# TensorE's loop body of the recurrent steps: sixteen steps and eight gate blocks in place of four and two

## The chip, the cores and the metric

The kernel runs on one core of a Trainium2 chip. Its time is the device time of one execution in microseconds (us), taken as the median of several. The core has five engines with a program each: TensorE (PE, matmuls; PEld is its weight load), VectorE (DVE), ScalarE (ACT), GpSimd (POOL) and SyncE (SP, which issues the DMAs here). They meet only through semaphores.

## The reference

Four layers in a row, each added to its input `x` of shape (4, 512, 512): batch, time, feature.

```python
x = x + attention(rms_norm(x) * (1 + scale) + shift)       # 16 heads, scale and shift from cond
x = x + gru(cond, x)                                        # hidden state starts at cond
x = x + causal_conv(x, cond)                                # depthwise, 4 taps
x = x + (causal_conv(x, cond) + b)

def cell(h, x):                                             # 512 steps, one after the other
    gi = x @ W_ih + b_ih
    gh = h @ W_hh + b_hh
    r = sigmoid(i_r + h_r); z = sigmoid(i_z + h_z)
    n = tanh(i_n + r * h_n)
    return (1 - z) * n + z * h
```

All is float32. The GRU can't be parallel in time: each of its 512 steps needs the state of the step before.

## The kernel before

**Stages.** The first block of the program does attention for the four batches, and the gate inputs `gi = x @ W_ih` for the first 128 time steps. It takes about 611 us. The second block does the 512 recurrent steps, and beside them the gate inputs for the other 384 time steps.

**A recurrent step.** TensorE multiplies the state `h` (128 partitions, 4 batches, 4 chunks of features) with `W_hh`, whose output columns are cut into four groups of 32 array columns (`NG`), in two halves `h` = 0 and 1 of the features. `products` (line 1100) issues the matmuls of one gate set, one half and two chunks: line 1106. A float32 matmul of the program appears in the profile as two matmuls with a weight load each, so 64 of the program are 128 in the trace. VectorE then transposes the sums (lines 962 and 968), ScalarE takes sigmoid and tanh (1064, 1070, 1075), VectorE scans (974 and 979) and so writes the next state, for which TensorE waits at the start of the next step (line 1111, `s_h`). ScalarE puts the input part of the next step into PSUM (`seed_rn`, `seed_z`), for which TensorE waits too. GpSimd does both convolutions two steps at a time.

**Gate blocks.** The remaining gate inputs are cut into `NBLOCKS` = 184 blocks of 104 columns. A block is computed in two halves, one behind each of two steps: `part(v, q)` (line 1126), eight matmuls of the program at line 1134, sixteen in the trace. SyncE brings each half's operands and counts them in `s_pair[v]`, VectorE takes the finished block (`take`) and counts `s_taken`. So the first 368 steps carry a part and the last 144 don't.

**Order and loops.** Every engine has its program written out by hand, in the order of the code. VectorE's 368 steps with blocks are written out in full, its last 144 are a loop of two steps a pass. ScalarE loops over sixteen steps, GpSimd over two. TensorE has two loops (`Fori` is a loop that the engine runs itself, with a counter in a register and a branch at the end of the body): the first over the steps with gate blocks (line 1143), the second over the rest (line 1149). Times of waits are computed from the counter (`e.snap` puts a value into a register).

Of the kernel before, what the change touches and what calls it, by code (L numbers as in the profile page):

```python
# [30 lines left out]
def build(nc, x, vec, w_emb, w_qk, w_v, w_out, w_rz, w_n, w_hh, b_rz, out):  # L31
    with ExitStack() as ctx:
# [820 lines left out]
        NBLOCKS = len(BLOCKS)  # L853
# [25 lines left out]
        def h_of(u, h):  # L879
            return hb[:, u, h, 0:HS].rearrange("p (i s) -> p i s", s=3)[:, :, 2]  # L880
# [11 lines left out]
        with nc.Block() as block:  # L892
# [200 lines left out]
            @block.tensor  # L1093
            def _(e):
                wv = whh[:].rearrange("p c (q G n) -> p c q G n", q=3, G=NG)

                def step(t, u):
                    half = (e.snap(2 * t + 1), e.snap(2 * t + 2))

                    def products(dst, gates, h, k2):  # L1100

                        n = len(range(3)[gates]) * 64
                        for k in (2 * k2, 2 * k2 + 1):
                            hv = h_of(u, k // 2).rearrange("p (b c) -> p b c", c=2)[:, :, k % 2]
                            for G in range(NG):
                                last = e.matmul(bank[dst[h]][32 * G:32 * G + B, 0:n], hv,  # L1106
                                                wv[:, k, gates, G, 64 * h:64 * h + 64],
                                                start=False, stop=k2 == 1 and k == C - 1, skip_group_check=True)
                        return last
                    rn, z = slice(0, 3, 2), slice(1, 2)  # L1110
                    e.wait_ge(st["s_h"], half[0])
                    e.wait_ge(st["s_seed_rn"], half[0])
                    products(RN, rn, 0, 0)
                    e.wait_ge(st["s_seed_rn"], half[1])
                    products(RN, rn, 1, 0)
                    e.wait_ge(st["s_h"], half[1])
                    products(RN, rn, 0, 1).then_inc(st["s_rn"], 1)
                    e.wait_ge(st["s_seed_z"], half[0])
                    products(RZ, z, 0, 0)
                    products(RZ, z, 0, 1).then_inc(st["s_z"], 1)  # L1120
                    products(RN, rn, 1, 1).then_inc(st["s_rn"], 1)
                    e.wait_ge(st["s_seed_z"], half[1])
                    products(RZ, z, 1, 0)
                    products(RZ, z, 1, 1).then_inc(st["s_z"], 1)

                def part(v, q):

                    if v == 0:
                        e.wait_ge(st["s_taken"], e.snap(q + 1))
                    e.wait_ge(s_pair[v], e.snap(q * 32 + 32))  # L1130
                    for k in (2 * v, 2 * v + 1):
                        for g in range(NG):
                            rows = slice(32 * g, 32 * g + 32)
                            last = e.matmul(bank[FB][rows, 0:BW], fixed[:, k, rows], moving[:, k, :],  # L1134
                                            start=k == 0, stop=k == C - 1)
                    last.then_inc(st["s_part"], 1)

                e.wait_ge(st["s_clear"], N_CLEAR)
                for b in RN + RZ:
                    for G in range(NG):  # L1140
                        last = e.matmul(bank[b][32 * G:32 * G + B, 0:P], zero[:, 0:B], zero, start=True, stop=True)  # L1141
                last.then_inc(st["s_open"], 1)
                with e.Fori(0, NBLOCKS // 2) as it:
                    for w in range(2):
                        q = e.snap(it * 2 + w)
                        for v in range(2):
                            step(q * 2 + v, v)
                            part(v, q)
                with e.Fori(NBLOCKS, T // 2) as it:
                    for v in range(2):  # L1150
                        step(it * 2 + v, v)
# [97 lines left out]
```

## Time and profile before

| | us |
|---|---|
| median of 3 runs | 2217.25 (2214.75 to 2222.03) |
| the profiled execution | 2214.76 |
| its span | 2212.8 |
| start of the first recurrent step | 617.87 |
| end of the first loop, start of the second | 1766.65 |
| TensorE busy | 2126.4 (96%) |
| VectorE, ScalarE, GpSimd busy | 1389.0, 1186.0, 1134.9 |

The span is the time from the first to the last instruction of the profiled execution. Busy time counts instructions that do work; register, branch and semaphore instructions aren't in it. A chain of waits is the work that ended last, followed back step by step; a piece called "issue" is time in which the engine waited for nothing that the profile shows. Instruction code has DMA queues of its own, which the page lists as "instruction".

### The profile page before, as it was taken

Reading aid. Unit: us, or ns where it says so; the run is one execution under the profiler, and the core shown is the slowest. Engines: PE = TensorE matmul, PEld = TensorE weight load, DVE = VectorE, ACT = ScalarE, POOL = GpSimd, SP = SyncE. Lnnn points to the kernel's source line nnn. Section 1 sums busy time; section 2 is a strip of 40 time slices with the busy share of each in tenths; the row PEclk is TensorE's granted clock in tenths of the full one; section 3 lists DMA queues with packets and bytes.
Section 4 is the critical chain, followed back from the end, with each engine's and each line's share of the span. In section 5 each row is a group of like instructions: output and inputs, shape, how many; then the busy total and the mean of one; then the engine's idle time right before and its main releaser. Section 6 shows DMA issues by size and latency. Waiting matters only on the chain.

```text
span 2212.8 us, 184515 instructions
## 1 busy us (share of the span) xinstructions
PE 2126.4 (96%) x76736; PEld 1590.4 (72%) x76736; DVE 1389.0 (63%) x5092; ACT 1186.0 (54%) x5992; POOL 1134.9 (51%) x3895
## 2 busy tenths in 40 slices
PE   6899999999989999999999999999999999999997
PEld 1222222222379999999999999999999988888886
DVE  1444443444257777777777777777777777777775
ACT  2344444443245555555555555555555555565554
POOL 1142432433135556555555656556555666666665
PEclk9899999999999999999999999999999999999999
DMA  6000000001022222112222221122221100000000
GB/s 247 1 1 1 1 1 1 1 20 59 32 58 51 54 54 51 49 51 53 68 52 52 54 53 49 50 70 55 50 51 50 48 5 24 6 6 5 5 7 19
DMA packets 159135, 86.69 MB, mean 39 GB/s; under 512 B 126016, under 2 KB 154944, under 8 KB 158272
## 3 DMA queue, kind: packets, MB, share of 16 engines
q1 hardware_dynamic: 158896, 83.42, 14.0%
q10 hardware_dynamic: 144, 2.10, 0.2%
q8 instruction: 48, 0.79, 0.1%
q14 instruction: 47, 0.39, 0.1%
HBM read 26.37 MB, written 12.58 MB: 18 GB/s over the span
## 4 chain that ended last, share of the span: by engine, by line
PE 66%; DVE 4%; issue 1%; DMA 1%; POOL 0%; ACT 0%; POOLq 0%; SPq 0%; DVEq 0%
PE ps L1106 60%; PE ps L1134 6%; DVE arena L962 3%; DVE arena L979 1%; DMA arena<-arena 1%; POOL arena L1171 0%; ACT ps L1039 0%; DVE arena L968 0%; PE ps L1141 0%; DVE arena L974 0%; POOL arena L1175 0%; POOL arena L1177 0%; DVE arena L1011 0%; DVE seq L992 0%; ACT arena L1070 0%
## 5 line engine op out<-in xcount | busy, mean ns | idle before, releaser
L1106 PE MATMUL ps<-whh,arena 128*4 128x128 f32 (+1 forms) x65536 | 1452.7, 246 | 34.2 <-DVE arena L979 27.2
L1106 PEld LDWEIGHTS ps<-whh,arena 128*4 128x4 f32 x65536 | 1310.3, 87 | 157.5 <-DVE arena L979 77.9
L962 DVE STREAM_TRANSPOSE arena<-ps 128x128 f32<-128x128 f32 x1024 | 434.7, 425 | 250.0 <-PE ps L1106 249.7
L1064 ACT ACTIVATE arena<-arena 128x8 f32<-128x8 f32 x1024 | 215.6, 211 | 649.5 <-DVE arena L962 628.0
L1171 POOL TENSOR_TENSOR arena<-tap,seq 128x32 f32<-128x32 f32 x1024 | 231.5, 257 | 256.3 <-DVE seq L992 256.3
L381 DVE TENSOR_REDUCE top<-ps 128x2 f32<-128x1024 f32 x128 | 150.8, 1220 | 257.5 <-PE ps L620 257.5
L979 DVE TENSOR_TENSOR_SCAN arena<-arena 128x24 f32<-128x24 f32 x1024 | 214.6, 210 | 144.8 <-ACT arena L1075 144.8
L1039 ACT ACTIVATE ps<-arena 128x128 f32<-128x128 f32 x1026 | 269.8, 263 | 0.7 <-PE ps L1141 0.7
L1171 POOL TENSOR_TENSOR arena<-tap,arena 128x32 f32<-128x32 f32 x1024 | 231.3, 257 | 66.8 <-POOL arena L1181 66.8
L968 DVE STREAM_TRANSPOSE arena<-ps 128x64 f32<-128x64 f32 x1024 | 253.2, 247 | 10.8 <-PE ps L1106 1.5
L523 PE MATMUL ps<-arena 128*32 128x512 f32 x2048 | 246.0, 600 | 11.5 <-POOL arena L214 11.5
L222 POOL TENSOR_TENSOR arena<-arena 128x2048 f32<-128x2048 f32 x16 | 72.8, 4551 | 337.0 <-ACT arena L296 337.0
L1075 ACT ACTIVATE arena<-arena 128x16 f32<-128x16 f32 x1024 | 222.7, 217 | 7.4
L974 DVE TENSOR_TENSOR_SCAN arena<-arena 128x16 f32<-128x16 f32 x1024 | 217.7, 213 | 4.8
L1175 POOL TENSOR_TENSOR arena<-arena 128x64 f32<-128x64 f32 x512 | 164.1, 320 | 95.2 <-POOL arena L1171 95.2
L1070 ACT ACTIVATE arena<-arena 128x8 f32<-128x8 f32 x1024 | 202.5, 198 | 1.1 <-DVE arena L968 1.1
L1134 PE MATMUL ps<-arena 128*32 128x104 f32 x5888 | 199.7, 253 | 1.7 <-DMA arena<-arena 1.7
L296 ACT ACTIVATE arena<-ps 128x1024 f32<-128x1024 f32 x128 | 124.1, 1022 | 133.5 <-PE ps L696 132.4
L523 PEld LDWEIGHTS ps<-arena 128*32 128x32 f32 x2048 | 60.2, 110 | 173.1 <-issue 173.1
L1043 ACT ACTIVATE ps<-arena 128x64 f32<-128x64 f32 x1026 | 181.6, 209 | 0.0
L1177 POOL TENSOR_TENSOR arena<-arena 128x32 f32<-128x32 f32 x512 | 129.0, 252 | 93.9 <-POOL arena L1175 93.9
L1134 PEld LDWEIGHTS ps<-arena 128*32 128x32 f32 x5888 | 131.8, 109 | 2.1 <-DMA arena<-arena 2.1
(89 smaller groups left out, 1298.9 us busy)
## 6 DMA issues: line engine op xcount, KB each, us to landing
arena<-arena SPq DMA_DIRECT2D x240, 104.0 KB, 2.1
arena<-seq SPq DMA_DIRECT2D x128, 104.0 KB, 2.1
arena<-gi_d SPq DMA_DIRECT2D x256, 32.0 KB
gi_d<-arena SPq DMA_DIRECT2D x108, 52.0 KB, 1.6
seq<-in_x SPq DMA_DIRECT2D x4, 1024.0 KB, 17.1
arena<-arena SPq DMA_DIRECT2D x32, 128.0 KB, 2.1
whh<-in_w_hh SPq DMA_DIRECT2D x1, 3072.0 KB, 21.2
arena<-seq SPq DMA_DIRECT2D x24, 128.0 KB, 2.2
```

What stands on the lines that cost most here:

```text
L523: last = e.matmul(dst[rows], w[:, rows], v, start=start, stop=stop)
L962: e.transpose(trn[:, h].rearrange("p q (i c s) -> p q c i s", c=2, s=2)[:, :, :, :, 0], bank[RN[h]][:, 0:P].rearrange("p (q c i) -> p q c ...
L968: e.transpose(trz[:, h].rearrange("p (i c) -> p c i", c=2), bank[RZ[h]][:, 0:64].rearrange("p (c i) -> p c i", c=2)).then_inc(st["s_tr"], 1)
L974: e.tensor_tensor_scan(pre[:, h], r_d0[:, h], trn[:, h, 1, 0:2 * NH], 0.0, ALU.mult, ALU.add).then_inc(st["s_pre"], 1)
L979: e.tensor_tensor_scan(hb[:, 1 - u, h, 0:HS], z_d0[:, h], hb[:, u, h, 1:HS + 1], 0.0, ALU.mult, ALU.add).then_inc(st["s_h"], 1)
L1039: e.activation(bank[RN[h]][:, 0:P].rearrange("p (q n) -> p q n", q=2), at(19456 + SLOT * s + 64 * h, 512).rearrange("p (q w) -> p q w", q= ...
L1064: e.activation(r_d0[:, h].rearrange("p (i s) -> p i s", s=2)[:, :, 1], trn[:, h, 0, 0:2 * NH].rearrange("p (i s) -> p i s", s=2)[:, :, 0], ...
L1070: e.activation(z_d0[:, h].rearrange("p (i s) -> p i s", s=3)[:, :, 2], trz[:, h, 0:NH], ACT.Sigmoid)
L1075: e.activation(hb[:, u, h, 1:HS + 1].rearrange("p (i s) -> p i s", s=3)[:, :, 0:3:2], pre[:, h].rearrange("p (i s) -> p i s", s=2)[:, :, 1 ...
L1106: last = e.matmul(bank[dst[h]][32 * G:32 * G + B, 0:n], hv, wv[:, k, gates, G, 64 * h:64 * h + 64], start=False, stop=k2 == 1 and k == C - ...
L1134: last = e.matmul(bank[FB][rows, 0:BW], fixed[:, k, rows], moving[:, k, :], start=k == 0, stop=k == C - 1)
L1171: last = e.tensor_tensor(prd[:, 0, w * k:w * k + w].rearrange("p (i s) -> p i s", s=2), tap[:, k], src[:, :, bass.ds(t + k, 2)], ALU.mult)
```

## The change

The first loop of TensorE's program runs over sixteen steps and eight blocks a pass, 23 passes, in place of four steps and two blocks, 92 passes. `step` and `part` and the numbers that they wait for are the same, and so is the second loop.

```diff
-                with e.Fori(0, NBLOCKS // 2) as it:
-                    for w in range(2):
-                        q = e.snap(it * 2 + w)
+                with e.Fori(0, NBLOCKS // 8) as it:
+                    for w in range(8):
+                        q = e.snap(it * 8 + w)
                         for v in range(2):
                             step(q * 2 + v, v)
                             part(v, q)
```

The programs of the other four engines are unchanged. On TensorE, before, this stands at the end of a pass, in and behind the fourth step (a row is a line, an instruction, its output and inputs, its shape and how often it follows itself; the semaphores are those of the text above):

```order
L1106 MATMUL ps<-whh,arena 4x128 x8
L1106 MATMUL ps<-whh,arena 4x64 [waits s_seed_z]
L1106 MATMUL ps<-whh,arena 4x64 x15
L1134 MATMUL ps<-arena 32x104 [waits s_pair1]
L1134 MATMUL ps<-arena 32x104 x7
L1143 REGISTER_ALU
L1143 COMPARE_AND_BRANCH
```

Behind the fourth step's block part the counter is raised and the branch goes back to the first step of the body.

On TensorE, now, at the same place, behind the fourth step:

```order
L1106 MATMUL ps<-whh,arena 4x128 x8
L1106 MATMUL ps<-whh,arena 4x64 [waits s_seed_z]
L1106 MATMUL ps<-whh,arena 4x64 x15
L1134 MATMUL ps<-arena 32x104 [waits s_pair1]
L1134 MATMUL ps<-arena 32x104 x7
L1111 ISA
L1106 MATMUL ps<-whh,arena 4x128 [waits s_seed_rn,s_h]
L1106 MATMUL ps<-whh,arena 4x128 x7
L1114 REGISTER_ALU
L1106 MATMUL ps<-whh,arena 4x128 [waits s_seed_rn]
```

The fifth step follows at once, and the counter and the branch stand behind the sixteenth. The written-out body is four times as long.

## Rows read from the trace of the kernel before

**Rows 1.** The page, part 1: busy us (share of the span) and instructions of each engine.

```profile
PE 2126.4 (96%) x76736; PEld 1590.4 (72%) x76736; DVE 1389.0 (63%) x5092; ACT 1186.0 (54%) x5992; POOL 1134.9 (51%) x3895
```

**Rows 2.** The page, part 5: groups by line, count | busy, mean ns | idle before.

```profile
L1106 PE MATMUL ps<-whh,arena 128*4 128x128 f32 (+1 forms) x65536 | 1452.7, 246 | 34.2 <-DVE arena L979 27.2
...
L1134 PE MATMUL ps<-arena 128*32 128x104 f32 x5888 | 199.7, 253 | 1.7 <-DMA arena<-arena 1.7
```

**Rows 3.** Busy us of PE, PEld, DVE, ACT, POOL; clock, DMA, GB/s; loop, passes 2 on.

```profile
633.95:1766.65 1132.70, 1125.78 (x52416) 1049.42 (x52417) 824.82 (x3459) 660.68 (x4004) 677.54 (x2729) 1.00 0.21 53
```

**Rows 4.** Timeline of TensorE, one pass: start us, us, instructions [idle before].

```profile
646.42 2.83 PE L1106 MATMUL ps<-whh,arena 128*4 128x128 f32 x128
...
649.47 2.83 PE L1106 MATMUL ps<-whh,arena 128*4 128x128 f32 x128
...
652.48 2.83 PE L1106 MATMUL ps<-whh,arena 128*4 128x128 f32 x128
...
655.49 2.84 PE L1106 MATMUL ps<-whh,arena 128*4 128x128 f32 x128
...
658.75 1.50 PE L1106 MATMUL ps<-whh,arena 128*4 128x128 f32 x48
```

**Rows 5.** Chain of waits, first pass of the first loop: start us, us, what.

```profile
617.87 4.58 PE ps L1106 x128
...
622.81 1.67 PE ps L1106 x69
624.48 0.02 issue
624.50 1.22 PE ps L1106 x54
625.72 0.35 PE ps L1134 x15
626.07 1.47 PE ps L1106 x52
627.54 0.47 issue
628.00 1.45 PE ps L1106 x70
...
630.83 0.69 issue
631.52 0.65 PE ps L1106 x16
```

**Rows 6.** DMA queues, first pass (617.87 to 633.95): packets, MB, share.

```profile
q8 instruction: 4, 0.07, 1.6%
```

**Rows 7.** DMA queues, the 91 passes that follow (633.95 to 1766).

```profile
q1 hardware_dynamic: 141235, 60.07, 21.0%
q14 instruction: 38, 0.31, 0.1%
```

**Rows 8.** DMA queues, start of the second loop (1766 to 1780).

```profile
q8 instruction: 2, 0.03, 1.1%
```

**Rows 9.** DMA queues, a stretch of the attention stage (100 to 400).

```profile
q8 instruction: 21, 0.34, 0.5%
```

**Rows 10.** Busy time of the same stretch, columns as in rows 3.

```profile
100.00:400.00 300.00, 292.81 (x2650) 80.86 (x2648) 127.81 (x138) 145.31 (x200) 105.96 (x30) 0.99 0.01 1
```

**Rows 11.** Busy time by stretch, around two idle times, columns as in rows 3.

```profile
66.40:69.47 3.07, 0.00 (x1) 0.03 (x1) 2.94 (x6) 0.00 (x0) 0.00 (x0) 0.86 0.00 0
68.60:78.80 10.20, 7.89 (x48) 2.55 (x52) 4.97 (x25) 2.54 (x3) 0.00 (x0) 0.50 0.00 1
610.85:615.49 4.64, 0.00 (x0) 0.00 (x1) 1.15 (x9) 1.17 (x5) 0.00 (x0) 0.92 0.21 40
615.49:621.50 6.01, 5.52 (x120) 3.89 (x124) 0.42 (x1) 2.54 (x8) 0.00 (x0) 0.50 0.53 92
621.50:633.95 12.45, 11.15 (x496) 9.91 (x489) 7.54 (x34) 6.09 (x39) 3.77 (x15) 1.00 0.13 35
```

## Prediction

> **What bounds the kernel now.** I read the page first: TensorE is busy 96% of the span [rows 1]. The reader is to see one engine that sets the pace and is almost never idle, so what happens between its instructions counts. The groups by line say of what its work in the recurrent steps consists: 65536 matmuls of line 1106 in 512 steps are 128 a step, 5888 of line 1134 in 368 steps are 16 a step [rows 2], and each has a weight load of its own. A step with a gate block's part is thus 288 matmuls and weight loads.
>
> Next comes the stretch of the loop that the change touches. From its second pass to its end, 91 passes take 1132.70 us [rows 3], 12.447 us for four steps. With the first pass, which begins at 617.87 [rows 5] and ends at 633.95, the loop takes 1148.8 us, half the span.
>
> Then the timeline of one pass. Steps start at 646.42, 649.47, 652.48, 655.49 and, across the branch, 658.75 us [rows 4]: 3.05, 3.01, 3.01 and 3.26 apart. So the branch with its register work costs 0.25 us of TensorE's time, and the rest of the loop is dense.
>
> Last, the very first pass, in which the body's code is new. Its chain has pieces called "issue", in which TensorE waited for nothing that the profile shows: one ends at 624.50, one at 628.00 (0.47 us long), one at 631.52 (0.69 us) [rows 5]. They lie 3.50 and 3.52 us apart, and some 121 matmuls of the chain (54, 15 and 52) with as many loads lie between two of them. In the same 16 us the instruction queue q8 moved 4 packets, 0.07 MB [rows 6]; in the 91 passes that follow q8 has no row [rows 7], and at the start of the next loop it moved 2 packets [rows 8]. In a stretch of the attention stage 21 packets go with 2650 matmuls and 2648 loads, 252 instructions to a packet, and 0.34 MB over 21 is 16 KB [rows 9, 10]. So TensorE's code comes in blocks of 16 KB, about 256 instructions; code that is there already is not fetched again; and new code comes one block at a time: a front that ran further ahead would have had the whole slow attention stage (a block in 14 us) to get there, and the first pass would not have stopped at each border.
>
> **The change, part by part.** Only TensorE's program changes. It does the same 184 blocks and 368 steps in 23 passes of sixteen steps in place of 92 passes of four.
>
> Removed: 69 branches at 0.25 us are 17.3 us, if nothing else happened.
>
> Added: size of the body. The present one has 4 x 288 = 1152 matmuls and loads and about 18 waits and register instructions, 1170 in all, 4.6 blocks. Where it begins within a block follows from the first pass: up to the stop at 624.48 stand 128 + 16 + 69 matmuls [rows 5], with their loads 426 instructions, and some five others, 431; one border lies 256 earlier, 175 after the body's start. The body starts some 80 instructions into a block and touches 5 blocks. The new body has 4608 and about 66, 4674 instructions; it ends 4754 instructions, 18.57 blocks, after the start of its first block, and touches 19.
>
> Whether 19 blocks stay at hand no row shows; 5 do. I take it that they don't: nothing in this trace was ever held in that amount, and a front that fetches only the next block looks like one over a small store. If blocks are dropped in the order in which they came, a store shorter than the body holds the wrong ones at each turn, and all 19 are fetched in every pass.
>
> The Trainium skill has a figure for this in "Runtime: NRT & Kernel Launch", section "Instruction fetch mechanics": 128 KiB for TensorE, 2048 instructions, in blocks of 16 KiB. The trace agrees on the block; that 8 blocks are the limit no row shows, and by it a body of 4674 would not fit.
>
> What a new block costs: TensorE uses up 256 instructions in 12.447 x 256 / 1170 = 2.72 us, and a new block comes 3.50 us after the one before. The fetch is the slower, so a pass goes at the pace of the fetches and each border costs 0.78 us. The bounds for a block: 2.72 us (the fetch just hidden), and 3.66 us (from the border 175 instructions into the first pass, which by that step's 4.94 us for 292 instructions lies at 620.8, to 624.5). I take 3.50, which the rows show twice. The work of the other engines lies beside this: VectorE, ScalarE, GpSimd and SyncE keep their programs, wait for TensorE's semaphores and have slack (the first three are busy 58 to 73% of this stretch [rows 3]); a wait for them of a tenth or three falls into the 0.78 us.
>
> What the jump back costs: its target is 18 blocks behind and has to be fetched with nothing beside it. No row has such a jump. The nearest is again one full fetch, 3.50 us. Below it stands 0.25 us, the jump of today. Above it: the block behind the loop was asked for when the last block was entered; the loop leaves that block after 146 instructions, 1.5 us, so if fetches queue up the jump waits the other 2.0 us and then 3.50, 5.5 us.
>
> The sum of a pass: 18 borders x 3.50 = 63.0 us and the last piece 1.5, together 64.5; 23 passes 1483.5. Jumps back: 22 x 3.50 = 77.0. Together 1560.5 us.
>
> The clock: after idle times of 3.07 and 4.64 us TensorE's granted clock was 0.50, the 1.2 GHz level, for 10 and for 6 us [rows 11]. A jump leaves it idle for about 3.5 us, so I expect such a fall in most passes. At that level a block takes 4.94 x 256 / 292 = 4.33 us in place of 3.50; over 6 us that is 1.4 blocks x 0.83 = 1.15 us a pass, 26 us in 23. Bounds: 0 (no fall) and 45 us (10 us in each pass).
>
> The loop then takes 1586.5 us and took 1148.8: +438 us. The profiled execution took 2214.76 us (the span and 2.0 outside it), which makes 2653 us; the median of the runs shown is 2.5 us higher than it, which I leave out. That is 20% slower.
>
> **A rule that speaks otherwise.** The same section of the Trainium skill says that the prefetch keeps ahead, because instructions are issued more slowly than blocks come, and that a taken branch to code that isn't there stalls. By the rows blocks came more slowly than they were used (3.50 against 2.72 us). By the rule alone the sum would be that of the second rival; by the rows it is mine.
>
> **The rivals.**
> 1. All 19 blocks stay at hand. Then 17.3 us go, and in the first pass 14 more blocks are new, at 0.78 us 10.9: 2214.8 - 17.3 + 10.9 = 2208 us. It decides as soon as the store is as long as the body. For it: no loop's code was fetched twice in this trace. Against it: that store is almost four times what is shown. This is the case on the other side, 0.3% faster, at the very border. Chance 0.06.
> 2. Borders are hidden once TensorE runs warm (the gaps belong to the cold start), and only the jump costs: 2214.8 - 92 x 0.25 + 22 x 3.50 = 2269 us, with clock falls 2295. For it: the clock was 0.50 in the first 3.6 us of that pass. Against it: the gaps grew, 0.02, 0.47, 0.69, after it had risen [rows 5, 11]. Chance 0.07.
> 3. The store keeps some blocks through the turn, say 8 of 19: 11 borders and the jump a pass, 23 x (11 x 0.78 + 3.5) - 23 = +255, 2470 us. Nothing speaks for a rule by which it would; nothing excludes it. Chance 0.05.
> 4. My forecast, every block in every pass: chance 0.82. Its own range: with 3.3 us a block and no fall of the clock 2539, with 3.6 us, queued jumps of 5.6 us and long falls 2759.
>
> **How the numbers follow.** The likeliest case gives 2653 us. The range runs from 2535 to 2765; it holds nearly all of that case and leaves out the three rivals, 0.18. A change under 0.3%, 7 us, can't be told from none. Rival 1 is split over that border: faster 0.03, same 0.03. All else is slower, 0.94.
>
> **What would show it.** q8 would have 480 to 510 packets and some 8 MB in place of 48 and 0.79. In the loop TensorE would have "issue" gaps of 0.7 to 0.8 us some 3.5 us apart, and every 66 to 71 us one gap of 3.5 to 5.5 us, behind which its granted clock is 0.50. Its busy share of the span would fall to about 80%. The stretch behind the loop, some 438 us, would be as before, and so would the counts of the groups. I am wrong if q8 stays near 60 packets (rival 1), if it has 480 and yet the steps between two jumps start 3.0 us apart (rival 2), or if it has 250 to 350 (rival 3). If the gaps at the borders are right and the jump's is 1 or 8 us, only that term was off.

## The result, and the profile after

The changed kernel takes 2768.3 us (median; 2766.4 to 2776.4) against 2217.0 (2214.8 to 2222.0), a ratio of 1.249 with a 95% interval of 1.246 to 1.252. The forecast was 2653, its range up to 2765, so the time lies 3 us outside.

The page after, parts 1, 3 and 4 (columns as in the page before; a queue's row is packets, MB, share):

```profile
PE 2240.8 (81%) x76736; PEld 1653.5 (60%) x76736; DVE 1368.4 (50%) x5092; ACT 1179.3 (43%) x5992; POOL 1135.5 (41%) x3895
...
q8 instruction: 502, 8.22, 1.3%
...
PE 56%; issue 16%; DVE 4%; ACT 1%; POOL 0%; POOLq 0%; DVEq 0%
```

TensorE is busy 81% of the span where it was 96% [rows 1], with the same 76736 matmuls. The instruction queue moved 502 packets in place of 48, and 16% of the chain that ended last is "issue". Per pass that is (502 - 48) / 23, about 20 packets: the 19 blocks of the body and the one behind it. Between any two jumps the trace has 20.

Busy time by stretch after, the whole first loop, and the second loop (columns as in rows 3):

```profile
618.66:2317.00 1698.34, 1254.09 (x52992) 1125.27 (x52992) 812.75 (x3492) 660.85 (x4046) 682.32 (x2745) 0.97 0.16 40
```
```profile
2316.80:2755.00 438.20, 409.35 (x18453) 363.58 (x18443) 311.35 (x1303) 259.96 (x1591) 268.24 (x1080) 1.00 0.04 8
```

The first loop takes 1698.3 us and took 1148.8, 549.5 more, which is all but 2 us of the difference of the spans (2764.4 less 2212.8, 551.6). The second loop takes 438 us as before.

The chain of waits after, around one jump back (start us, us, what), to be held against the first pass before [rows 5]:

```profile
743.86 2.83 PE ps L1106 x128
746.69 1.22 issue
747.91 0.56 PE ps L1134 x16
748.47 2.40 PE ps L1106 x109
750.87 1.03 issue
751.91 0.45 PE ps L1106 x18
...
754.87 0.89 issue
755.76 0.78 PE ps L1106 x30
...
758.73 1.23 issue
759.96 0.77 PE ps L1106 x22
...
762.15 3.26 issue
765.41 4.48 PE ps L1106 x128
769.89 0.36 PE ps L1134 x16
770.25 1.65 PE ps L1106 x69
771.89 0.18 issue
772.07 1.22 PE ps L1106 x54
...
775.11 1.02 issue
```

The pattern of the first pass before is now that of every pass: a stop after each 256 instructions. Here the stops end 4.00, 3.85 and 4.20 us apart (747.91, 751.91, 755.76, 759.96). Behind 759.96 TensorE works off what the loop has in its last block, other engines finish the step's chain, and the rest is the jump: the first step of the next pass starts at 765.41. By the trace's record of the branch, TensorE hangs on it for 4.07 us here and for 4.32 in the mean of the 22 jumps. Its first 213 matmuls stand before the stop at 771.89, as they did at 624.48.

The granted clock, in a part of the time at the jump, and behind it (columns as in rows 3):

```profile
761.20:765.20 4.00, 0.30 (x15) 0.07 (x3) 1.01 (x5) 1.09 (x7) 1.72 (x7) 1.00 0.20 46
765.70:769.10 3.40, 3.40 (x89) 3.05 (x84) 0.69 (x3) 0.38 (x2) 1.52 (x7) 0.50 0.19 33
```

After the idle 4 us the clock was at the 1.2 GHz level for 3.4 us here. It fell in all 22 passes that begin with a jump, in 13 of them for 3.4 us and in 9 for 6.8.

### The profile page after: what moved, and what is told of

Same layout as the page of the kernel before. It is cut to its first block, busy times and chain, and to the rows that moved or that the text cites. A ratio compares the mean times of both kernels' runs of the same rounds, so it can differ in the third digit from the quotient of the medians.

```text
span 2764.4 us, 184377 instructions
## 1 busy us (share of the span) xinstructions
PE 2240.8 (81%) x76736; PEld 1653.5 (60%) x76736; DVE 1368.4 (50%) x5092; ACT 1179.3 (43%) x5992; POOL 1135.5 (41%) x3895
## 3 DMA queue, kind: packets, MB, share of 16 engines
q1 hardware_dynamic: 158896, 83.42, 11.3%
## 4 chain that ended last, share of the span: by engine, by line
PE 56%; issue 16%; DVE 4%; ACT 1%; POOL 0%; POOLq 0%; DVEq 0%
PE ps L1106 51%; PE ps L1134 5%; DVE arena L962 3%; DVE arena L979 1%; ACT ps L1039 0%; ACT arena L1070 0%; ACT arena L1075 0%; DVE arena L968 0%; DVE arena L974 0%; ACT arena L1064 0%; PE ps L1141 0%; POOL arena L1171 0%; DVE arena L1011 0%; POOL arena L1175 0%; POOL arena L1177 0%
## 5 line engine op out<-in xcount | busy, mean ns | idle before, releaser
L1106 PE MATMUL ps<-whh,arena 128*4 128x128 f32 (+1 forms) x65536 | 1581.9, 250 | 420.9 <-issue 369.1
L1106 PEld LDWEIGHTS ps<-whh,arena 128*4 128x4 f32 x65536 | 1378.7, 88 | 586.4 <-issue 464.6
L1134 PE MATMUL ps<-arena 128*32 128x104 f32 x5888 | 227.7, 256 | 51.5 <-issue 51.5
L974 DVE TENSOR_TENSOR_SCAN arena<-arena 128x16 f32<-128x16 f32 x1024 | 195.7, 191 | 4.7
L1134 PEld LDWEIGHTS ps<-arena 128*32 128x32 f32 x5888 | 151.5, 111 | 60.9 <-issue 60.9
L523 PEld LDWEIGHTS ps<-arena 128*32 128x32 f32 x2048 | 60.2, 110 | 173.2 <-issue 173.2
```

What stands on the lines that cost most here:

```text
L523: last = e.matmul(dst[rows], w[:, rows], v, start=start, stop=stop)
L974: e.tensor_tensor_scan(pre[:, h], r_d0[:, h], trn[:, h, 1, 0:2 * NH], 0.0, ALU.mult, ALU.add).then_inc(st["s_pre"], 1)
L1106: last = e.matmul(bank[dst[h]][32 * G:32 * G + B, 0:n], hv, wv[:, k, gates, G, 64 * h:64 * h + 64], start=False, stop=k2 == 1 and k == C - ...
```

## The experiments

Theory A: code comes in blocks of 256 instructions, one at a time, slower than TensorE uses them up; the store holds 8 blocks; a body that needs more is fetched anew in each pass. Its rivals are that only the jump costs, that the store is larger, and, for the size of the effect, that the kernel's own transfers slow the fetch.

**How many blocks stay: e1, e2, e11, e3, e4.** The six-step body needs one block written out behind the loop, since 184 is not a multiple of 3:

```diff
-                with e.Fori(0, NBLOCKS // 8) as it:
-                    for w in range(8):
-                        q = e.snap(it * 8 + w)
+                with e.Fori(0, NBLOCKS // 3) as it:
+                    for w in range(3):
+                        q = e.snap(it * 3 + w)
                         for v in range(2):
                             step(q * 2 + v, v)
                             part(v, q)
+                for v in range(2):
+                    step(2 * (NBLOCKS - 1) + v, v)
+                    part(v, NBLOCKS - 1)
```

> Body of six steps and three blocks, 61 passes, and the 184th block written out behind the loop: 1754 instructions that begin some 80 slots into a fetch block, so 8 blocks are touched and a ninth is asked for while the eighth runs. Theory A (the store holds 8 blocks, and the oldest goes first, the block fetched ahead included): each pass loses its first block to the ninth, and the whole body is fetched anew each time: per pass 7 borders x 3.8 + 0.6 + 4.3 = 31.5 us against 18.65, so 2217 + 61 x 12.9 = about 3000 us, q8 some 550 packets. Rival B (the store is larger, 9 to 18 blocks, and only the 19 of the changed kernel do not fit): no refetch, 31 branches fewer at 0.25 us, about 2210 us, q8 some 55 packets.

e2 and e11 are e1 with tiny matmuls at the start of the program, 46 and 30 of them, which move the body within its blocks:

```diff
                 e.wait_ge(l_vec, 16)
+                for _ in range(46):
+                    e.matmul(bank[OB][0:B, 0:B], vecT[:, 0, 0:B], vecT[:, 0, 0:B], start=True, stop=True)
                 e.wait_ge(l_emb, 16)
```

> The same body of six steps, with 46 tiny matmuls (184 instructions) added at the program's start, where TensorE waits for its first weights, so that the body begins about 8 slots into a fetch block and touches 7 blocks; with the one fetched ahead that makes 8. Theory A (8 blocks in all): all of it fits, no block is fetched twice, 2217 - 31 x 0.25 = about 2209 us, q8 some 56 packets. If the store holds only 7, it is as slow as the run beside it. Rival B: the same 2209, and the run beside it too. A difference between the two runs is a matter of blocks alone, since the instructions of the loop are the same.

> The body of six steps again, with 30 tiny matmuls (120 instructions) at the program's start, so that it begins some 200 slots into a block: it touches 8 blocks as in e1, but the eighth holds 162 of its instructions and not 42. In e1 only every other pass fetched its code anew (30 long jumps in 60). Theory A (the request for the ninth block pushes the first out, and in e1 the jump often came before that request was made, since only 42 instructions lay between): here every pass fetches all 8 blocks, 7 x 3.8 + 0.6 x 2.72 + 4.6 = 33 us a pass, 2217 + 61 x 14.2 = about 3080 us. Rival (something else drops the first block every other time): about 2570 us again.

e3 and e4 have 4 and 1 in place of 8 in the changed lines.

> Body of eight steps and four blocks, 46 passes: 2338 instructions, 10 blocks touched. Theory A (store of 8): all fetched in every pass, 9 borders x 3.8 + 1.2 + 4.3 = 39.7 us against 24.9 of now: 2217 + 46 x 14.8 = about 2895 us, slower than the sixteen-step body although it has more straight code, q8 about 510 packets. Rival B (store of 10 to 18): 2217 - 46 x 0.25 = 2206 us. Rival C (the jump back alone costs, borders are cheap once warm): 2217 - 23 + 45 x 4.3 = 2388 us.

> Body of two steps and one block, 184 passes, 586 instructions, 3 blocks touched. By every theory all code stays at hand and only the price of the branch shows: 92 more of them at 0.25 us, 2217 + 23 = 2240 us.

| run | steps a pass | blocks touched | us | ratio (95%) | q8 packets | long jumps of all |
|---|---|---|---|---|---|---|
| before | 4 | 5 | 2220.3 | 1 | 48 | 0 of 91 |
| e4 | 2 | 3 | 2231.2 | 1.005 (1.0035 to 1.0066) | 46 | 0 of 183 |
| e2 | 6 | 7 | 2216.5 | 0.998 (0.9973 to 0.9991) | 54 | 0 of 60 |
| e1 | 6 | 8 | 2569.5 | 1.157 (1.156 to 1.159) | 323 | 30 of 60 |
| e11 | 6 | 8 | 3005.7 | 1.356 (1.353 to 1.358) | 593 | 60 of 60 |
| e3 | 8 | 10 | 2849.1 | 1.283 (1.281 to 1.285) | 548 | 45 of 45 |
| after | 16 | 19 | 2768.3 | 1.249 | 502 | 22 of 22 |

The queue's row on the pages of e2, e1 and e11, whose loops hold the same instructions:

```profile
q8 instruction: 54, 0.88, 0.2%
```
```profile
q8 instruction: 323, 5.29, 0.9%
```
```profile
q8 instruction: 593, 9.72, 1.4%
```

The store holds 8 blocks, one of which the request ahead takes: a body in 7 blocks runs without a fetch, the same body in 8 doesn't, and the difference is 789 us between e2 and e11. Rivals B and C of e3 are out: C had 2388 us. Fewer steps a pass cost more once the body doesn't fit (e11, e3, after: 3006, 2849, 2768), and with them goes the number of jumps (60, 45, 22); e3 and after have the same 414 borders inside their passes, and 45 jumps of 4.62 us against 22 of 4.32. e1 missed: I expected about 3000 us, and every other pass ran from the store. e11 took 3006 us where I expected 3080.

The traces show what makes the difference. In e1 the body leaves 38 instructions in its eighth block (by the start at 76 that e12 shows below), in e11 158. Here are a pass of e1 with stops and the one behind it, first their rows of the instruction queue (663.9 to 694; from 694 to 712.4 the queue has no row), then two places of the chain:

```profile
q8 instruction: 9, 0.15, 2.4%
```
```profile
692.94 0.97 issue
693.91 0.23 PE ps L1109 x2
...
713.61 3.72 issue
```

Behind the last stop, at 693.91, the branch follows after 0.19 us. No packet for a ninth block is seen, and the branch finds its target. The pass behind it, 18.4 us, fetches nothing: all 8 blocks are there. It has no stop at its end, and there the packet of the ninth block does come, 0.44 to 0.59 us after the branch begins; this branch doesn't find its target (4.49 to 4.99 us, 4.74 in the mean). So it goes in all of the 60 jumps, in turn. In e11 the branch comes 1.19 us after the last stop, the ninth block's packet starts about when the branch does (0.04 us before it in the mean), and no jump finds its target. That the request for the ninth block throws out the first is how this fits together; the trace has no record of what the store drops.

**The jump back: e5, e6.** e5 writes all 184 blocks out (`for q in range(NBLOCKS)`, no loop). e6 adds a hint to the changed kernel:

```diff
-                with e.Fori(0, NBLOCKS // 8) as it:
+                with nc.Fori(0, NBLOCKS // 8, engines=bass.OrderedEngineSet([e.engine]), hint_back_edge=True) as it:
```

> The 368 steps with blocks are written out, with no loop and no jump: 106.6 thousand instructions, 417 fetch blocks. Theory (the fetch of one block at a time sets the pace, 3.8 us a block in the changed kernel's run): 416 x 3.8 = 1581 us for the stretch, so 2768 less 22 jumps of about 4.4 us = 2670 us, q8 about 465 packets, and no fall of the clock inside. Rival (the borders are slow only because each pass begins with a miss and a half clock, straight code would catch up): the stretch comes near 368 x 3.04 = 1119 us, 2190 us in all.

> The changed kernel with a hint at the top of the body which names the branch at its end, so that the branch's target can be fetched before it is taken. If the hint works across 18 blocks, the jump's 4.4 us shrink to under 1 and the kernel takes 2768 - 22 x 3.8 = about 2685 us; the borders stay at 3.8. If the hint is lost on the way or the fetched block is pushed out again: 2768.

e5 took 2609.6 us (ratio 1.176), with 460 packets. Straight code does not catch up, so rival 2 of the prediction is out. Its chain, from the middle of the stretch (start us, us, what):

```profile
1501.91 0.88 issue
1502.80 2.43 PE ps L1109 x95
...
1505.57 0.69 issue
1506.27 0.38 PE ps L1137 x5
1506.64 2.55 PE ps L1109 x116
1509.19 0.91 issue
1510.11 0.29 PE ps L1109 x6
```

The stops are there without any loop: they end at 1502.80, 1506.27 and 1510.11, and the packets start 3.70 us apart in the mean. Both this and the 60 us that e5 is below what I expected say that a block takes 0.1 to 0.15 us less here than in the changed loop. e6 took 2731.6 us, 37 less than the change, where I expected 83 less: the record of the branch shows 2.60 us a jump in place of 4.32, 38 us in 22 jumps. Its chain at a jump:

```profile
762.49 1.69 issue
764.19 4.48 PE ps L1106 x128
```

What a jump consists of can be read from the packets of q8 around it. Here are the queue's rows at one jump of the changed kernel (760.5 to 765) and at one of e15 (688 to 692), the same loop with only 14 instructions in its last block:

```profile
q8 instruction: 2, 0.03, 3.5%
```
```profile
q8 instruction: 1, 0.02, 1.6%
```

In the changed kernel one packet is that of the block behind the loop, which starts 0.09 us after the branch (means of 22 jumps); the target's starts 1.02 us after the branch, takes 1.89, and TensorE goes on 1.40 after its end: 4.32 us with rounding. In e15 there is only the target's packet. It starts 1.03 us after the branch, takes 1.10, and TensorE goes on 1.40 later: 3.53 us. So the block behind the loop doesn't hold back the start of the target's packet, it makes it slower, by 0.8 us; in e12, where it starts 0.80 us ahead of the branch, the target's takes 1.22 us, and in e1, 0.52 us behind the branch, 2.01. In e6 a pass has 19 packets in place of 20, the one of the block behind the loop is missing, and the target's starts 0.10 us after the branch and takes 1.06. The hint thus saves the 0.9 us until the packet starts and the 0.8 by which it was slower, and leaves the rest.

**The time of a block: e7 to e10.** e7 brings the operands of the gate blocks once, e8 also loads the ring only for the first sixteen steps:

```diff
                     weights, src = wn[:, ks, P * b:P * b + P], seq_cb[:, ks, c, PAD + a:PAD + a + BW]
+                    if q:
+                        e.sem_inc(s_pair[v], 32)
+                        return
...
-                    load_ring(e, first // HALF % 2, first)
+                    e.sem_inc(s_ring[first // HALF % 2], 16 * NG)
```

> The changed kernel, but the operands of the gate blocks are brought once, for block 0, and all later blocks use them again (their values are wrong by that); of the loop's small packets most are gone, the ring loads and stores stay. Theory A (a block took 3.8 us and not 3.5 because its packet stands behind the kernel's own transfers): intervals fall to about 3.45, 23 x 18 x 0.35 = 145 us less, about 2620 us. Rival (3.8 is what the fetch costs in this stretch, whatever else moves): 2768.

> As the run beside it, and the ring of gate inputs is loaded only for the first sixteen steps and used again after (values wrong by that). What stays are the stores of the blocks. Theory A: intervals fall to about 3.35, about 2580 us. Rival: 2768.

They took 2742.9 and 2743.3 us, 25 us less than the change, not the 145 and 190 of theory A. Between packet starts stand 3.79 and 3.78 us in the mean, 3.86 in the changed kernel: the transfers taken out (q1 has 44656 and 35728 packets in place of 158896) cost 0.07 us a block. The stores of the blocks stay in both.

e9 and e10 put the fetch by itself behind the last step of the kernel before:

```diff
+                with e.Fori(0, 10) as it:
+                    for j in range(1168):
+                        G = j % NG
+                        e.matmul(bank[5][32 * G:32 * G + B, 0:64], zero[:, 0:B], zero[:, 0:64], start=True, stop=True)
```

> The kernel before, and behind its last step TensorE runs 10 passes over a body of 1168 matmuls of the 4x64 form (4672 instructions, as many as the changed body) that wait for nothing and multiply zeros into a bank that nobody reads. This measures the fetch by itself: no waits, hardly any transfers. In the changed kernel the interval between two fetches was 3.86 us, 3.6 to 3.7 at borders in the first two thirds of a step and 4.0 to 4.2 near its end. Theory A (the waits for the state, at a step's start, hold up the request for the next block): all intervals here 3.55 to 3.65, no pattern, the jump back 4.2 us; a pass 18 x 3.6 + 5 = 70 us. Rival B (3.86 is what a fetch costs): 3.86 throughout, 74 us a pass. Rival C (the pattern belongs to the blocks and their place in memory): intervals of 3.6 and 4.1 here too.

> The same body cut into sixteen steps of 72 matmuls; at a step's start TensorE waits for VectorE, which is let go by the step's 48th matmul and then makes two transposes (some 0.9 us). Theory A: at borders that lie in the last third of a step the next request comes later, by 0.3 to 0.5 us, at the others not; mean 3.7 to 3.8. Theory B or C: as the run beside it, the step's start makes no difference.

The chain of e9, in one of its passes:

```profile
2279.17 2.81 PE ps L1155 x128
2281.99 0.93 issue
2282.92 1.97 PE ps L1155 x128
2284.89 1.50 issue
2286.39 1.97 PE ps L1155 x128
2288.36 1.51 issue
2289.86 1.97 PE ps L1155 x128
```

128 matmuls and 128 loads, then a stop, and so on: a block is 256 instructions to the last one. The starts are 3.47 to 3.75 us apart; between the 199 packets the mean is 3.60 us and the median 3.51, 5% are below 3.34 and 5% above 4.04. That is the fetch with no wait and next to no transfer beside it, as theory A had it. It has three parts, by the traces' means: 1.16 us from TensorE's going on in a new block to the start of the next one's packet, 1.06 for the packet, 1.38 from its end until TensorE goes on. Rival B (3.86 here too) and C (a pattern) are out; the means by place in the pass lie between 3.50 and 3.70, but for the first behind the jump (3.20). A pass took 71.7 us, where 70 were expected, and the jump 3.39, not 4.2. (e9 and e10 were run once each, 2918.5 and 2915.7 us; what is read here is inside their traces.) In e10 the mean is 3.66; borders that lie 200 to 250 instructions into a step have 3.79, the others 3.57 to 3.73. The effect of a wait is there but smaller than the 0.3 to 0.5 us I expected.

**Where a border lies: e15.** The changed kernel with 32 of the tiny matmuls.

> The changed kernel with 32 tiny matmuls (128 instructions) at the program's start: the same body begins half a block later. In the changed kernel the intervals between fetches were long (4.0 to 4.2 us) behind the blocks 6 to 8 and 15, 16 of a pass, whose borders lie in the last third of a step. If the place in the step decides (each border lies 36 instructions earlier in its step than the one before), the long ones move 3 to 4 blocks on, to some 2 to 4 and 10 to 12. If the block's place in memory decides, they stay. The sum hardly changes: 2768, with one block more or less 3.8 us x 23 = up to 90 us either way; by the count the body now ends at 204 + 4674 = 4878, 19.05 blocks, so it touches 20: some 2780.

It took 2786.5 us, where 2780 was expected. The mean intervals behind the fetches 2 to 4 of a pass (the first is the one behind the jump's) were 4.09, 3.91 and 3.96 us, and behind 11 to 13 3.99, 3.81 and 3.94; between the groups 3.6 to 3.8. In the changed kernel the long ones are 6 to 8 (4.03, 4.03, 4.01) and 15 to 17 (4.17, 4.04, 3.98). So the time of a block goes with its place in the step. One long interval doesn't fit, the 11th with 3.98; it is 3.72 and 3.61 in e7 and e8, so it belongs to the kernel's own transfers. In e5, where each block runs once, the same is seen, but weaker: 3.60 to 3.66 us at borders 75 to 200 instructions into a step, 3.76 to 3.79 behind that. Of the three parts of a fetch only one grows at those places of the changed kernel: the next block's packet starts 1.44 to 1.64 us after TensorE went on, and 1.12 to 1.37 at the others that follow a full stop. What holds the request up isn't shown: e10 speaks for the wait at the step's start, and for a part of it only.

**A version that beats both: e12, e13, e14.** e2 is 3.8 us faster than before by 31 branches fewer, e4 10.9 slower by 92 more. That looks like 0.12 us for each branch removed or added, which I took as its price. In the turned loop the branch stands inside a step, behind its first two groups of matmuls:

```diff
+                step(0, 0, rest=False)
                 with e.Fori(0, NBLOCKS // 2) as it:
                     for w in range(2):
                         q = e.snap(it * 2 + w)
                         for v in range(2):
-                            step(q * 2 + v, v)
+                            step(q * 2 + v, v, first=False)
                             part(v, q)
+                            step(q * 2 + v + 1, 1 - v, rest=False)
```

(`rest=False` issues `products(RN, rn, 0, 0)` and `products(RN, rn, 1, 0)` with their waits, `first=False` the others; behind the loop the begun step is completed, one more step follows, and the second loop begins two steps later. e14 is this. e12 and e13 are the same with three blocks a pass and 28 and 30 tiny matmuls at the start.)

> A version meant to beat both: six steps a pass in 7 blocks (28 tiny matmuls at the program's start place the body), and the loop is turned, so that the branch stands behind the first two groups of matmuls of a step (64 instructions of the 128-column form) and not behind a gate block part at the step's end. Where the branch is now, TensorE has about 28 instructions in its queue, 0.2 us, and the branch with its register work takes 0.47. Theory (with 64 wide instructions queued, 0.8 us, the branch is hidden): 60 x 0.25 = 15 us less than the run e2, ratio to before 0.991, 2200 us. Rival (the queue is no fuller there): 0.998, as e2.

> e12 again with the body at the right place. Its first long stop in each pass lay 2 instructions behind the body's first one: the body began at slot 253 and touched 8 blocks, since my count of the start (80) was 4 too high. Now 30 tiny matmuls in place of 28: slot 5, 7 blocks, no refetch, q8 some 55 packets. The price of a branch by e2 and e4 is 0.12 us (3.8 us for 31, 11 for 92) and not 0.25. If turning the loop hides it, 60 x 0.12 = 7 us less than e2: ratio to before 0.995. If it does not, 0.998. If a branch there costs more, since its register work now stands inside a step, 1.000 or above.

> The kernel before with its loop turned in the same way (branch behind the first two groups of matmuls of a step), 92 passes of four steps, nothing moved otherwise: the price of the branch alone. Hidden: 92 x 0.12 = 11 us less, ratio 0.995. Not hidden: 1.000.

e12 took 3046.5 us, with 593 packets and 60 long jumps in 60 passes: it began at slot 253, three before a block's end, and touched 8 blocks. My count of 80 for the start was 76 in truth. e13, two tiny matmuls more, took 2195.7 us (0.989, 0.9875 to 0.9908), and e14 2189.9 us (0.9866, 0.9850 to 0.9883): the best version, 31 us below the kernel before where 11 were expected, and simpler than e13, which gains nothing from its longer pass. The step starts of e14, by its timeline, and behind them those of the kernel before, in the same 14 us of the loop:

```profile
1001.92 2.83 PE L1109 MATMUL ps<-whh,arena 128*4 128x128 f32 x128
...
1004.94 2.83 PE L1109 MATMUL ps<-whh,arena 128*4 128x128 f32 x128
...
1007.94 2.84 PE L1109 MATMUL ps<-whh,arena 128*4 128x128 f32 x128
...
1010.96 2.84 PE L1109 MATMUL ps<-whh,arena 128*4 128x128 f32 x128
```
```profile
1000.44 2.83 PE L1106 MATMUL ps<-whh,arena 128*4 128x128 f32 x128
...
1003.47 2.83 PE L1106 MATMUL ps<-whh,arena 128*4 128x128 f32 x128
...
1006.70 2.83 PE L1106 MATMUL ps<-whh,arena 128*4 128x128 f32 x128
...
1009.80 2.83 PE L1106 MATMUL ps<-whh,arena 128*4 128x128 f32 x128
...
1012.86 1.40 PE L1106 MATMUL ps<-whh,arena 128*4 128x128 f32 x44
```

In e14 the steps are 3.00 to 3.02 us apart here. In the kernel before, the step across the branch takes 3.23 and those behind it 3.10 and 3.06. Its branch is recorded at 1006.20; the first matmul behind it starts 0.31 us after the last one ahead of it, while around e14's branch at 999.39 no two matmuls start more than 0.11 us apart.

The price of a branch follows from whole passes. A pass of e2 (six steps) takes 18.49 us in the mean and one of the kernel before (four) 12.45; the two steps more are 3.02 us each, and 12.45 less 4 x 3.02 leaves 0.37 us for the branch, 34 us in 92. A pass of e14 takes 12.12, so its branch costs about 0.04 (a pass of e4, 6.31, leaves 0.27 for the branch), and 92 x 0.33 = 30 us is what e14 gains. The 0.12 was too low because e2 pays for its longer body elsewhere: its loop is only some 7 us shorter by the traces, where 31 branches are worth 11. Its first six steps and the two written out behind the loop take 4 us more than in the kernel before; there the code is new, 54 packets in all against 48. Whether it is the wide matmuls in the queue or the distance from the wait at the step's start that hides e14's branch, no run separates.

## Why the prediction came out as it did

The mechanism was right, and the forecast failed by the size of a term, the time of a new block; the jump was sized too low as well, and the clock too high.

- *Every block in every pass.* Right: 502 packets where 480 to 510 were forecast. The limit that no row of before showed is now shown: 7 blocks and the one ahead.
- *Stops at the borders, 0.7 to 0.8 us, some 3.5 us apart.* They are there, but 0.9 to 1.2 us long and further apart. This is the step that failed: "I take 3.50, which the rows show twice". The loop's 1698.3 us, less 22 jumps of 4.32 and 23 last pieces of 1.5, leave 3.79 us for each of its 414 borders. 0.29 x 414 is 120 us. Two stops were read as if a fetch had one length. e9 shows what it has: a median of 3.51 us, which the two stops met, but 3.60 in the mean with a spread from 3.34 to 4.04, and a sum over 414 borders goes by the mean. To that come 0.07 us for the transfers (e7) and, as an estimate from the long intervals of the changed kernel (six of the 19 in a pass, some 0.3 us above the others), about 0.1 for the borders near the end of a step. My own upper bound of 3.66 was below the measured mean, too.
- *The jump, 3.50 us.* Measured 4.32, between the bounds of 3.50 and 5.5: 18 us more. The step that was wrong is that the target is fetched "with nothing beside it": the packet of the block behind the loop is under way, and the target's takes 1.89 us with it and 1.10 without (e15, where the jump takes 3.53). The upper bound, fetches that queue up one behind the other, is out: the target's packet starts 1.02 us after the branch either way.
- *The clock, 26 us.* It falls as forecast, in each pass, but that costs little or nothing: behind the jump shown above, at half clock for 3.4 us, TensorE comes from its first matmul (765.41) to the second border (772.07) in 6.66 us, less than two borders at 3.79. A block at half clock needs about as long as the fetch beside it, so the stop is only shorter (0.18 us at 771.89). The sum counted both, 26 us too many.
- *Together.* 120 + 18 - 26 = 112, the 112 by which the loop's 1698.3 exceed the 1586.5 forecast. That it comes out even says nothing, since the 3.79 is what remains of the loop; it holds whatever the clock cost. The packets' mean of 3.86 is measured apart from it and is over all 19 intervals of a pass, the one behind the jump (4.06) included. A pass is 74.0 us, not the 66 to 71 forecast. Of the 115 us by which the time is off, the other 3.5 lie outside the loop (2) and between the profiled execution and the median (2).
- *17.3 us for 69 branches.* It was not part of the sum. At the 0.37 us that a branch costs between two steps it would be 25. Nothing of it can be seen in the changed kernel, whose passes go at the pace of the fetches.
- *The stretch behind the loop, the counts of the groups.* As forecast.

Rival 1 (all blocks stay) and rival 2 (only the jump costs, 2269 us) are out by the packets and by e5. Rival 3 (some blocks stay through the turn) is out by the 20 packets of each pass; what stays in e1, every second time, is the whole body.

## What to carry to other kernels

A loop of TensorE is cheap as long as its body fits the instruction store with one block to spare, here 7 blocks of 256 instructions, where a float32 matmul of the program takes four. The count must start from where the body begins in its block: the same loop took 2216 us with 46 tiny matmuls 600 us earlier and 3006 with 30. A branch that finds its target still cost 0.37 us between two steps and about 0.04 behind 64 wide matmuls and loads inside a step; it is worth trying to put it there.

## What the runs showed of the hardware that I had not expected

- A body in exactly 8 blocks whose last holds 38 instructions runs from the store in every other pass (e1: 30 long jumps in 60). A branch that comes 0.19 us after the last border is reached leaves no packet for the ninth block; in a pass without stops the packet comes.
- A jump to a block that isn't there took 3.53 us with one packet on the instruction queue (e15) and 4.32 with two (after).
- The time of a fetched block depends on where in the step its border lies, by 0.4 us and more in four kernels (after, e3, e7, e15) and by some 0.15 in straight code (e5).
- Straight code isn't safe either: written out without a loop, these steps are 18% slower than in a loop of four (e5).
